# Maxima of the attention scores in spare rows of the block-diagonal queries: one product per score step

## What is computed

```python
x = x + L0_xattn(layernorm(x), ctx)          # cross attention, 77 context rows
# L0_ffn(hs = layernorm(x)):
Q = (hs @ q_w + q_b).reshape(B, S, 16, 8)[..., :4]      # 16 heads, 4 of 8 columns are used
K = (hs @ k_w + k_b).reshape(B, S, 16, 4)
V = (hs @ v_w + v_b).reshape(B, S, 16, 4)
attn = softmax(Q @ K.T / sqrt(4))
mla_out = concat(attn @ V, zeros) @ o_w + o_b
probs = softmax(mla_out @ router_w + router_b)           # top 2 of 8 experts
h1 = gelu(mla_out @ w1[e] + b1[e]); h2 = h1 @ w2[e] + b2[e]
x = x + hs + 0.3 * sum_e(combine[e] * h2[e])
x = x + L1_xattn(layernorm(x), ctx, ...)                 # bidirectional attention flow
x = x + L1_ffn(layernorm(x), ...)                        # expert 7, weighted by its probability
```

## Time and profile before

| | |
|---|---|
| median of 3 runs | 164.38 us (164.29 to 164.40) |
| the profiled execution, its time | 165.29 us |
| its span | 163.5 us |
| mean granted clock of PE | 0.979 |
| PE busy | 149.5 us (91%), 1305 instructions |
| DVE busy | 109.6 us (67%) |
| ACT busy | 107.2 us (66%) |
| POOL busy | 42.8 us (26%), 126 instructions |

### The profile page before, as it was taken

The page is one execution under the profiler, slowest core; times in us unless marked ns, Lnnn a source line. Parts: engine busy times, 40 slices in busy tenths (PEclk is TensorE's granted clock), DMA queues, the critical chain, the costliest instruction groups (busy, mean ns, idle before and its releaser), DMA issues.

```text
span 163.5 us, 3969 instructions
## 1 busy us (share of the span) xinstructions
PE 149.5 (91%) x1305; PEld 120.3 (74%) x1313; DVE 109.6 (67%) x408; ACT 107.2 (66%) x238; POOL 42.8 (26%) x126
## 2 busy tenths in 40 slices
PE   7798964899999999999999999999899989999891
PEld 5567843565755566557899799998799969779780
DVE  2766999849844785661087728986747897687744
ACT  3687795446586778789859635655954595666480
POOL 7997005220220259446000000540003200310100
PEclk9999999579999999999999999999999999999999
DMA  4439304533486320310100000000000000000022
GB/s 114 135 100 327 106 2 86 115 88 66 100 170 184 50 46 6 53 18 6 34 0 0 4 0 0 0 4 0 2 4 0 0 0 6 0 0 2 4 64 64
DMA packets 11071, 8.02 MB, mean 49 GB/s; under 512 B 1867, under 2 KB 10155, under 8 KB 11051
## 3 DMA queue, kind: packets, MB, share of 16 engines
q1 hardware_dynamic: 11051, 7.76, 19.5%
HBM read 5.26 MB, written 1.70 MB: 43 GB/s over the span
## 4 chain that ended last, share of the span: by engine, by line
PE 51%; issue 27%; DVE 10%; POOL 4%; ACT 2%; DMA 2%; ACTq 1%; SPq 1%; POOLq 1%; DVEq 0%
PE ps L1080 49%; DMA x<-in_x_dram 2%; DVE qbd L858 2%; POOL rstd L566 2%; DVE stats L769 2%; ACT pr L623 1%; DVE nmax L864 1%; POOL xn L560 1%; ACTq L56 1%; POOL f_lo L536 1%; DVE xn L784 1%; PE ps L1102 1%; DVE vpad L977 1%; PE ps L1268 1%; DVE mv L773 1%
## 5 line engine op out<-in xcount | busy, mean ns | idle before, releaser
L702 ACT ACTIVATE vpad<-ps,b1o 128x256 f32<-128x256 f32 (+1 forms) x48 | 23.6, 543 | 16.1 <-PE ps L1080 16.0
L1080 PE MATMUL ps<-w2s,vpad 128*128 128x128 f32 x256 | 31.5, 276 | 0.2 <-DVE vpad L977 0.2
L1080 PEld LDWEIGHTS ps<-w2s,vpad 128*128 128x128 f32 x256 | 30.0, 192 | 0.8 <-issue 0.5
L864 DVE TENSOR_REDUCE nmax<-ps 128x4 f32<-128x512 f32 x32 | 21.3, 685 | 9.6 <-PE ps L1080 9.3
L977 DVE SCALAR_TENSOR_TENSOR vpad<-ps,comb,vpad 128x128 f32<-128x128 f32 x64 | 18.4, 341 | 10.5 <-PE ps L1080 10.3
L652 ACT ACTIVATE pexp<-ps 128x512 f32<-128x512 f32 x32 | 18.5, 595 | 8.4 <-PE ps L1080 5.5
L1080 PE MATMUL ps<-ao,w_lo 128*128 128x256 f32 (+1 forms) x48 | 16.5, 358 | 0.3 <-ACT vpad L702 0.3
L1080 PEld LDWEIGHTS ps<-kst,qbd 128*128 128x128 bf16 x128 | 9.2, 104 | 9.4 <-issue 7.7
L1080 PE MATMUL ps<-kst,qbd 128*128 128x128 bf16 x128 | 12.7, 231 | 2.8 <-DVE nmax L864 2.6
L566 POOL TENSOR_TENSOR rstd<-veps,power 128x2 f32<-128x2 f32 (+1 forms) x6 | 4.8, 808 | 39.4 <-DVE veps L779 39.4
L1080 PE MATMUL ps<-ao,w_hi 128*128 128x256 f32 (+1 forms) x48 | 14.6, 318 | 0.0
(11 more groups left out here) (224 smaller groups left out, 328.1 us busy)
## 6 DMA issues: line engine op xcount, KB each, us to landing
w1s<-in_L_ffn_w_dram SPq DMA_DIRECT2D x1, 1024.0 KB, 5.5
kst<-scratch_k SPq DMA_DIRECT2D x8, 72.0 KB
qbd<-scratch_q SPq DMA_DIRECT2D x8, 72.0 KB
w1s<-w1s SPq DMA_DIRECT2D x8, 64.0 KB
x<-in_x_dram SPq DMA_DIRECT2D x2, 192.0 KB, 3.4
scratch_q<-part SPq DMA_DIRECT2D x2, 144.0 KB, 2.6
scratch_k<-part SPq DMA_DIRECT2D x2, 144.0 KB, 2.5
wqv<-in_L_xattn_W_qv_dram SPq DMA_DIRECT2D x1, 256.0 KB, 3.5
```

Of the source, the lines that this page charges most:

```text
L702: act.activation(hT[:, k % 2, c, 0:n], ps[:, h1_bank(k, c), 0:n], ACT.Gelu, bias=b1o[:, e, c:c + 1]).then_inc(s["gelu_ok"], 1)
L864: dve.tensor_reduce(nmax[:, b, g, :], ps[:, n % 2, :].rearrange("p (j t) -> p j t", t=S), axis=AX.X, op=ALU.max, negate=True).then_inc(s[" ...
L1080: return nc.tensor.matmul(dst, lhsT, rhs, start=start, stop=stop)
```

## The change

The maxima ride in the product that s2 needs anyway. The spare rows of a lane move from its end to its start (`SPARE` = 8 rows, then 24 rows of parts; selection and transfers are shifted). In `kst` the spare rows are now one instead of zero: ACT adds the column `spare1` as it writes (Identity with a bias), and fills the later two thirds with the word `pair1`, whose two halves are the bf16 number 1. In `qbd` the spare rows have to be zero as long as s1 reads them, so DVE's sixteen copies become products with the column `used1`. After s1 has read them and the maxima are split and transposed, POOL writes the three rows of parts from `mT` into the first three spare rows of the diagonal blocks (the new function `max_rows`, stage `mrow:b`, four copies, one per group, each for its own lane of partitions, ahead of them a memset of one column, `fence`). s2 waits for it (`mrow_ok`) and is one product. `selg`, its mask and its reduction are gone. `hot:b,k` is a new stage of one product of ones in the bank of `av`. And the whole table `plan` is written in another order, of which the diff shows two rows only: the same stages, and those named here.

```diff
@@ constants and tiles
-MUSED = PARTS * GROUPS
-MROWS = P
+SPARE = ROWS - USED
+PAIR_OF_ONES = 1.0 + 0x3F80 / 2 ** 23
...
-        mT = sb("mT", [MROWS, 2, LANES, S], BF16)
-        selg = sb("selg", [MROWS, GROUPS, S], BF16)
+        mT = sb("mT", [P, 2, LANES, S], BF16)
+        spare1 = sb("spare1", [P, 1])
+        used1 = sb("used1", [P, 1])
+        fence = sb("fence", [P, 1])
+        pair1 = sb("pair1", [P, 1])
@@ plan
-            s2:0,0 s2:0,1 s1:1,2 p1_T2:2 av:0,0 s1:1,3 s2:0,2 p1_split:2 z_v:2 p1_qk:2 s2:0,3 p1_v:2 mT:1 av:0,1 av:0,2 s1:2,0
...
+            z_identb p1_norm1:2 s1:1,1 p1_T2:2 s2:0,0 s1:1,2 s2:0,1 msp:0 av:0,0 ctxw:0 s1:1,3 a_q:3 p1_qk:2 s2:0,2 p1_split:2
...
@@ SP, parts
-                    rows_ = slice(ROWS * j, ROWS * j + USED)
+                    rows_ = slice(ROWS * j + SPARE, ROWS * (j + 1))
@@ POOL, split_max
-                m = msp[:, b % 2, :].rearrange("p (j c) -> p j c", j=LANES)[:, :, 0:MUSED].rearrange("p j (q g) -> p j q g", g=GROUPS)
+                m = msp[:, b % 2].rearrange("p j (g c) -> p j c g", g=GROUPS)[:, :, 0:PARTS, :]
...
+            def max_rows(b):
+
+                a = did(pool.memset(fence[:, :], 0.0))
+                after(a)
+                pool.wait_ge(s["mT_ok"], b + 1)
+                for g in range(GROUPS):
+                    r = slice(ROWS * g, ROWS * g + PARTS)
+                    last = pool.tensor_copy(qbd[r, g, :, b * S:(b + 1) * S].bitcast(FP32), mT[r, b % 2, :, :].bitcast(FP32))
+                last.then_inc(s["mrow_ok"], 1)
+                pool.wait_ge(s["mrow_ok"], b + 1)
@@ ACT
-                zero(kst[:, :, :].rearrange("p g t -> p (g t)").bitcast(FP32).rearrange("p (g t) -> p g t", g=GROUPS)[:, :, T // 2:], GROUPS).then_inc(s["zero_k"], 1)
+                fill(kst[:, :, :].rearrange("p g t -> p (g t)").bitcast(FP32).rearrange("p (g t) -> p g t", g=GROUPS)[:, :, T // 2:], GROUPS, pair1).then_inc(s["zero_k"], 1)
...
-                act.activation(kst[:, g, 0:T], ps[:, ROW_BANKS[g], :], ACT.Copy).then_inc(s["kq_ok"], 1)
+                act.wait_ge(s["spare1_ok"], 1)
+                act.activation(kst[:, g, 0:T], ps[:, ROW_BANKS[g], :], ACT.Identity, bias=spare1[:, 0:1]).then_inc(s["kq_ok"], 1)
...
-                    act.wait_ge(s["s2_ps"], GROUPS * (b - 1))
+                    act.wait_ge(s["mrow_ok"], b - 1)
@@ DVE
-            def sel_groups():
-                dve.wait_ge(s["selm_ok"], 1)
-                dve.tensor_reduce(selg_c[:, :], selg_m[:, :, :], axis=AX.X, op=ALU.add).then_inc(s["selc_ok"], 1)
+            def spare_words():
+                dve.wait_ge(s["ident_ok"], 1)
+                a = did(dve.tensor_reduce(spare1[:, :], ident[:, :].rearrange("p (j x) -> p j x", j=LANES)[:, :, 0:SPARE], axis=AX.XY, op=ALU.add))
+                after(a)
+                dve.tensor_scalar(out=used1[:, :], in0=spare1[:, :], scalar1=-1.0, scalar2=1.0, op0=ALU.mult, op1=ALU.add).then_inc(s["spare1_ok"], 1)
...
-                    last = dve.tensor_copy(qbd[r, g, j, 0:FRONT[0][1] * S], kst[r, g, T // 2:T])
+                    last = dve.tensor_scalar(out=qbd[r, g, j, 0:FRONT[0][1] * S], in0=kst[r, g, T // 2:T], scalar1=used1[r, 0:1], scalar2=None, op0=ALU.mult)
@@ PE
+            def keep_clock(bank):
+
+                v = ones[:, :].bitcast(BF16)
+                mm(ps[:, bank, 0:2 * P], v[:, 0:P], v[:, :])
...
+            def hot(b, k):
+
+                av_bank_free(b)
+                keep_clock(5 + b % 2)
...
             def s2(b, g):
...
-                pe.wait_ge(s["mT_ok"], b + 1)
-                pe.wait_ge(s["selg_ok"], 1)
+                pe.wait_ge(s["mrow_ok"], b + 1)
...
-                mm(dst, kst[:, g, cols_of(b)], qbd[:, g, :, cols_of(b)], True, False)
-                mm(dst, selg[:, g, :], mT[:, b % 2, :, :], False, True).then_inc(s["s2_ps"], 1)
+                mm(dst, kst[:, g, cols_of(b)], qbd[:, g, :, cols_of(b)]).then_inc(s["s2_ps"], 1)
```

More of the change, by code:

```diff
@@ L569, in _ @@
             run({"z_sel": select, "z_wqk": pick_q, "z_q": queries, "z_identb": ident_b,
-                 "z_mask": group_mask, "z_msp": maxima, "z_v": values,
-                 "z_selg": group_rows, "z_den": denominators, "z_const": constants, "msp": split_max, "w1": split_w1, "fw1": split_f1,
+                 "z_msp": maxima, "z_v": values,
+                 "z_den": denominators, "z_const": constants, "msp": split_max, "mrow": max_rows, "w1": split_w1, "fw1": split_f1,
                  "p4_ln": lambda u: rstd_of(2, u), "x2b": x2_bias, "p5_ln": lambda u: rstd_of(3, u)})
@@ L764, in _ @@
             dve.memset(nil[:, :], 0.0).then_inc(s["ones_ok"], 1)
+            dve.memset(pair1[:, :], PAIR_OF_ONES).then_inc(s["ones_ok"], 1)
             def var_of(i, src, group):
@@ L1070, in _ @@
                  "p1_norm": lambda u: norm_of(0, x0, fseqs(u), u), "p1_norm1": lambda u: norm_of(1, x1, fseqs(u), u),
-                 "p1_split": split, "p1_v": add_v, "selg": sel_groups, "s1": s1, "norm": norm, "oT": wo_T, "fr": router_fold, "fb": bias_fold, "ao2": low_part, "router": router, "combine": combine, "x2_init": x2_start, "rows": rows_of,
+                 "p1_split": split, "p1_v": add_v, "spare": spare_words, "s1": s1, "norm": norm, "oT": wo_T, "fr": router_fold, "fb": bias_fold, "ao2": low_part, "router": router, "combine": combine, "x2_init": x2_start, "rows": rows_of,
                  "acc": acc, "p4_ln": ln2, "p4_norm": lambda u: norm_of(2, x2, seqs(u), u), "p4_simd": sim, "p4_nbm": nbmax,
```

112 lines of the change are left out of this document (53 added, 59 removed).

## The result

The changed kernel takes 170.84 us in the median of four runs (168.83 to 172.26), the kernel before 164.39 in the same session (164.29 to 164.7); the ratio is 1.028 (95%: 1.023 to 1.032). By the medians it is slower by 6.5 us, where I had forecast 3.3 us less. Two of the four runs, in which TensorE's clock was granted at 0.948 and 0.959 in the mean of the span, took 172.26 and 171.97 us, and the ratio counts only the other two (168.83 and 169.72 us, both at 0.975), which are 4.5 to 5 us slower than before. The profiled execution is the fastest of the four, 168.83 us with a span of 167.0 us: 3.5 us of span more than before.

The account below looks back on a forecast made before the run. PE was taken to bound the attention from 34.6 to 75.9 us, DVE before 29 us. Second products -6.0 and masked copies +2.7 sum to -3.3 us, from the median 164.38 to 161.1 us; range 157.1 to 164.2.

Parts of the forecast that it names:

- the masked copies: DVE's sixteen `qbd` copies become multiplications by `used1`: 385 instead of 219 ns each, all on the path, +2.7 us.
- The second products: Each of 32 s2 steps loses its second product on PE: -6.0 us, with ends 0 and -7.3.
- ACT's 74%: ACT's share from 34.6 to 75.9 us; staying at it would leave no room for gain, 89% was held possible.
- Rival (a): The masked copies in `qbd` keep the speed of the plain ones: 158.4 us; chance 30%.
- POOL's loop: From one `msp` to the next through PE, ACT and POOL's copies: 4.4 us, covered by PE, costed at nothing.
- Rival (b): POOL's loop becomes the pace, between `mT` b and `msp` b+1: 5.2 us a round, slower at 165.8 us; chance 13%.
- the transfers: Sequences 2 to 4 through DRAM, `stack_in1` complete at about 39.0 us: no cost, but no slack.
- the reordered second half: From 75.9 us on the same products in another order: could give or take about 1 us, taken as 0.
- the clock to fall as before: The four fillers `hot` are too short against 2.58 us of PE idle time, so the clock's dip stays.
- Rival (c): The fillers and the earlier s1 keep PE's clock at 2.4 GHz: 1.7 us gained, 159.4 us; chance 7%.

Follow-up runs that it names:

- e6: The kernel before without its 32 second products, so the maxima are left out of the exponent; 161.91 us, ratio 0.985.
- e14: e13 with plain copies in place of the sixteen masked multiplications, so the mask of the spare rows is left out; 166.21 us.
- e16: e13 without POOL's four copies per sequence and their memset, so the maxima are left out of the exponent; 166.37 us.
- e2: The changed kernel in the order of the kernel before, `mrow` right behind `msp`, without the fillers `hot`; 177.82 us.
- e11: The changed kernel with one signal per copy of the maxima, the old second-half order, eight fillers before 14 us and 31 from 24 to 32 us; 167.5 us.
- e13: e11 with projection and split of sequences 2 to 4 ahead of `s1:0,0`, and ACT's two fills ahead of the first `mT` copy; 166.22 us.
- e4: The changed kernel with the order of the kernel before from the first expert product (`gelu:0,0`) on; 171.84 us.
- e10: The kernel before with 28 more fillers where PE is idle from 23 to 29 us; 164.29 us, ratio 0.993.
- e1: The kernel before (old algorithm, `selg` stages kept) in the changed kernel's order, with the four fillers `hot`; 171.64 us, ratio 1.032.
- e3: The changed kernel without `max_rows`, s2 waiting for `mT` only, so the maxima are left out of the exponent; 169.49 us.
- e17: e13 with the very first score product and its exponential ahead of the transposes of sequences 5 to 7; 166.61 us.

## Why the prediction was wrong, step by step

Two steps failed. One was a term too large, the other a term that the sum didn't have; the first alone, with the masked copies at the 0.9 us that they cost, would have left a gain of some 2 us, and it is the second that made the kernel slower.

- **"The second products ... I stay near PE's count and take -6.0 us": the first step that failed.** It was read from a PE share of 99% and one look at ACT's share. e6 measured it without any of the costs: -3.7 us by its profile, -2.7 in the median. I had written a test: at ACT's 74% "there would be no room for any gain". It stayed at 73% in the changed kernel and rose to 78% in e6. My argument, that ACT's share was low because PE led, most likely left out that between two instructions of ACT there lies not PE's work alone but the whole way over DVE, POOL and PE's queue.
- **"I take +2.7 us" for the masked copies: too high, in the other direction.** They took 278 ns, not 385: 16 x 59 ns = 0.9 us, and e14's profile gives 0.9. The first `msp` therefore stands at 28.69 us and not near 30.6. Rival (a) was nearer than my forecast on this term. The Trainium skill, "VectorE: DVE Perf Modes", perf-mode tier table, has both kinds at the same rate; measured is 278 against 219 ns for the same 32x256, so they are neither equal nor at the speed of the fp32 rows from which I worked out 385.
- **"I cost it at nothing" for POOL's loop: right, but for one order only.** Copies 0.40 (forecast 0.41), tightest round 4.28 us (forecast 4.4), and e16 finds 0.1 to 0.7 us. In the old order the kernel with this way is 13 us slower (e2). I priced the loop and not the order that had to be written around it. Rival (b) has the right sign and the wrong place: from 35 us on PE waited 0.9 us for these copies.
- **"No cost, but no slack either" for the transfers: the end was right by luck, and the cost was not nothing.** `stack_in1` was there at 39.1 (forecast 39.0). But the writes began at 27.39 us (forecast 29.0) and the reads at 32.75 (forecast 34.4), and from there to the last packet it took 5.8 us (38.5) instead of 4.6, as it does in some executions and not in others; two errors cancelled. PE waited 0.79 us at this point, and in e11 1.66 us. I had seen that the reads wait for ACT's fill, and took it for harmless because the loop was as late. e13 moves both, and gains 1.3 us on e11 in the median.
- **"I take 0" for the reordered second half: 1.0 us was lost**, in each of the eight profiles with that order (88.5 to 88.7 us, against 87.5 to 87.7 in ten with the old one; e4 has a dip there), at the edge of my +-1.
- **"I expect the clock to fall as before": it did in the profile, and fell more in other runs.** That is about 1.5 us of the median (170.84 against 169.3 for the two runs at 0.975). Rival (c) gave 1.7 us for holding the clock; on the kernel before it gave 0.4 in the median (e10), and 1.3 in the faster group of its runs.
- **The new order of the attention, at nothing: the second step that failed.** The sum has no term for it at all; I had taken it as free because it was the same stages. With the old algorithm it costs 5.2 to 7 us (e1). Of this 1.0 us is the second half, and 4.1 us lie between the first split of the maxima and the first expert product (31.12 to 83.13 in e1, 27.93 to 75.88 before), of which some 0.6 may be the clock (6.8 us at half clock in e1's profile, 5.6 before). In the changed kernel the part that I can name stands before 39 us. The first score product stands 2.85 us later, of which 0.9 are the masked copies; the rest has two causes that end together: POOL's four copies (1.8 us from 31.36 us on, with one signal behind the last) and a transpose put ahead, which waits for a normalisation on DVE (32.10). Taking away the one alone leaves the other (e3, e16: from the transposed maxima to the product 2.9 instead of 3.2 us, and 2.6 instead of 2.9). e17 has the transpose away and waits for the first copy alone, 1.6 us from the transposed maxima to the product, and then the next `msp` is late. Which waits behind 39 us make up the remainder stays open.

## What to carry to other kernels

A share of 99% on one engine says that the others are hidden, not how deeply: before you price the removal of its work, run the kernel without that work and nothing else changed, and take that as what the idea can give in the order that stands. Where an order is written by hand over five engines, a longer way for one value is paid in the order that makes room for it; list what each engine's first instruction behind a long wait is, and which transfers or fills stand behind it (here a fill of 1 us behind a wait of 6 us). And cost a reordered stretch by measuring it with the old algorithm (e1), since its price was larger than that of any instruction. Where fillers hold the clock, look again at what they stand before each time the order changes: in e13 they held back the maxima by 0.9 us.

## What was unexpected of the hardware

A DVE instruction with two operands in SBUF is held up by a POOL instruction that began before it. The product `un` times `rden` takes 0.28 us alone; beside a split of `w1s` on POOL, from the timelines of the changed kernel, DVE's row first:

```profile
74.46 0.83 DVE L879 TENSOR_TENSOR aoT<-un,rden 128x128 f32<-128x128 f32 x1
...
74.37 0.76 POOL L520 TENSOR_TENSOR w_lo<-w1s,w_hi 128x256 fp32r<-128x256 f32 x1
```

POOL's ends at 75.13, DVE's at 75.29, 0.15 us later. Six of the eight products of the changed kernel began while POOL was at work on SBUF, and all six end 0.14 to 0.15 us behind the end of a POOL instruction, whether that one held them for 0.04 us (68.07, beside a copy of the maxima) or for 0.55 (74.46). The Trainium skill, "SBUF — State Buffer", section "SBUF: two separate sides", says that the two engines share one pair of ports as an exclusive lock: of a DVE instruction with two SBUF inputs and a POOL instruction that reads SBUF, the one that starts first holds it, and the other waits. The trace agrees for POOL starting first; the mean of these eight instructions rose from 314 to 465 ns. No instruction is shown to wait for one of the eight in the changed kernel's trace.

The second surprise is that a kernel at full clock can still have two levels of time. In e10 a stretch of 5.6 us went from 1.2 to 2.4 GHz, and the kernel gained 0.4 us in the median, but its runs stand 1 us apart in two groups. What varies with the execution is the transfers of sequences 2 to 4: eight reads of 72 KB take 4.5 to 4.8 us from the first issue to the last packet in eight profiles, and 5.3 to 5.8 in eleven. In the changed kernel's profile (5.8 us) the last of them trickle in, with a DMA share of 0.03 from 38 to 39 us, while in the kernel before (4.6 us) the share falls from 0.65 to 0 at 35. What decides it stays open.
